# Two state decays ahead of the Silu in idle PSUM banks, with earlier x loads, earlier rows, the inverse deviation in PSUM and a hinted loop branch

## The chip, the cores and the metric

One NeuronCore of a Trainium2 chip runs the whole program, in fp32. The metric is the device time of one execution in microseconds (us). The kernel before takes 10367.23 us (median of 3 runs, 10365.2 to 10386.27).

## The reference

The input is 32 images of 256 x 256 positions with 4 features. What matters here is layer 0's mixer, a two-way Mamba. Behind it follow an expert layer, an attention and a routed MLP, which the second phase of the kernel computes.

```python
h = _L0_tok_ref(x, W, b)                      # tokens: 256 of width 256
h = concatenate([cls_tok, h], axis=1)         # 257 positions
h = h + _L0_attn_ref(_layernorm(h), ...)      # below

def _mamba_block(x, ...):                     # four of them, d=512, 16 states
    xn = _layer_norm(x, g, b)                 # 1 / sqrt(variance + eps)
    xs, z = split(xn @ in_w)
    xc = silu(conv(xs) + conv_b)              # 4 taps, depthwise
    delta = softplus(xc @ xd_w @ dtp_w + dtp_b)
    Bm, Cm = xc @ xB_w, xc @ xC_w
    dA = exp(delta[..., None] * A)            # the decays
    dBx = (delta * xc)[..., None] * Bm
    y = scan(h = dA * h + dBx; y = sum(h * C)) + D * xc
    return y * silu(z) @ out_w + x
fwd = blk(blk(x, 0), 1); bwd = blk(blk(x[:, ::-1], 2), 3)[:, ::-1]
concatenate([fwd, bwd]) @ merge_w
```

## The kernel before

Two phases run one after the other. `mamba_phase` computes tokens and the mixer, `tail_phase` the rest. The change lies in the first alone.

**Tiling.** The 32 images go in 16 groups of 2 (NB). A group needs four blocks, and each block of one group is a *job*: 64 jobs. The 512 channels are 4 chunks of 128 partitions (CI), so a job has 64 states (chunk c, state n; s = 16 c + n), each a tile of 128 x 512. A job is walked in 32 *units* u of two states (2u and 2u + 1). While a job's states are scanned, the engines also finish the job before (output projection) and prepare the next: normalisation, input projection, convolution, Silu, the projection xp, step sizes dt0 to dt3.

**Who does what.** ScalarE makes the decay of each state (`decays`, line 776) into one of two PSUM buffers (NDP = 2), so decay s waits for the scan of state s - 2. GpSimd multiplies B by u (`b_times_u`, lines 544 and 547) and for every fourth state C by h (line 556). VectorE scans (lines 978 and 982) and multiplies the other states by C (line 998), turns x - mean into the normalised value (`normalize`, line 944, which multiplies the tile cen by the tile rstd), and multiplies turned-back rows by the gate (`output`, line 1018). TensorE adds the states up in turned form (`add_state`, line 1233), turns a chunk's rows back (`channel_rows`, line 1245), and does all products (`product`, line 1117) and the tokens (`tokens`, line 1134). SyncE issues the DMAs.

**What sets the order.** Every engine has its own written order, `period(g, jj, first, last)`, with fixed units for each step (`gates_at`, `y_at`, `silu_at`, `norm_at`, CONV_AT = 15). The convolution's Silu (line 698, with a table load ahead and one behind, line 699) stands at u = 24 of ScalarE, after decay 51. The rows of chunks 0, 1 and 2 (y0, y1, y2) are turned back at u = 12 or 14, 18 and 25, at the head of the unit behind its two additions; VectorE takes them a unit later, between its scans. The products xp stand at u = 25 of TensorE, dt0 and dt1 at 26 and 27; ScalarE copies xp (line 707) at u = 26, starts softplus (lines 717 and 718) at 27 and takes logarithms (line 730) at 29 and 30; VectorE uses the first of these at u = 30 (line 953).

**Banks.** All products share three PSUM banks `w_ps` in turns. The turns are written in a list of keys (`preparation`, `one_job`, `later_keys`): turn i takes banks 0 and 1 when even, 2 and 1 when odd, y rows only one bank. A product waits until turn i - 2, for its second bank sometimes turn i - 1, is read (`bank_free`). `work_full` and `work_read`, one semaphore each for either parity, count the turns.

**The inverse deviation.** `inverse_deviation` (lines 656 and 659) takes a logarithm of the variance from PSUM into rstd in SBUF, tells that the turn "var" is read, and takes an exponential of half of it.

**Tokens.** In the job jj = 2 of a group (15 times) x of the next group is loaded (`load_x`, eight loads of 256 KB through two buffers, issued after the gates' products and the next weights) and turned into tokens at units 10 to 13 of TensorE: t0, then "var", y0, t1. ScalarE copies t1 (line 623) at u = 14, ahead of decay 32.

**The loop.** Job 0 stands ahead, then each engine has a loop of 15 passes over the four jobs jj = 1, 2, 3, 4; the last three jobs stand behind it (`run`).

Of the kernel before, what the change touches and what calls it, by code (L numbers as in the profile page):

```python
# [5 lines left out]
ALU = mybir.AluOpType  # L6
# [6 lines left out]
NB = 2  # L13
# [13 lines left out]
BLOCK_OF_JOB = (0, 2, 1, 3)  # L27
CONV_AT = 15
EPS = 1e-5
LOG_EXP = "natural_log_exp_and_others"  # L30
# [5 lines left out]
def mamba_phase(nc, a, h_mid, bc_dram, diag_dram, skip_dram):  # L36
# [13 lines left out]
    def preparation(jj, tokens):  # L50

        first = norm[:2] + ["t0"] + norm[2:] + ["t1"] if tokens else norm
        steps = first + conv + ["xp", "dt0", "dt1", "dt2", "dt3"]
        return [(name, 4 if name in ("t0", "t1") else jj) for name in steps]
# [98 lines left out]
    with ExitStack() as ctx:  # L153
# [94 lines left out]
        rstd_ready = sem("rstd_ready")  # L248
        xhat_ready = sem("xhat_ready")
        xn_ready = sem("xn_ready")  # L250
# [62 lines left out]
        def run(eng, lead_in, period, tail):  # L313

            lead_in()
            period(0, 0, True, False)
            with eng.Fori(0, GROUPS - 1) as g:
                for jj in (1, 2, 3, 4):
                    period(g, jj, False, False)
            for jj in (1, 2, 3):  # L320
                period(GROUPS - 1, jj, False, jj == 3)
            tail(GROUPS - 1)
# [4 lines left out]
        def _(sp):  # L327
# [63 lines left out]

            def load_x(g, jj):

                for n in range(8):
                    c, b, half = n // 4, n // 2 % 2, n % 2

                    if positive(g * 8 + 8 * (jj // 4) + n - 1):
                        sp.wait_ge(x_used, g * 8 + 8 * (jj // 4) + n - 1)
                    src = a["x"][bass.ds(g * NB + (jj // 4 * NB + b), 1), half * P:(half + 1) * P, c * P:(c + 1) * P, :]
                    sp.dma_start(x_in[:, n % 2, :, :], src.rearrange("o i j f -> (o i) j f")).then_inc(x_loaded[n % 2], 16)  # L400
# [33 lines left out]
            def period(g, jj, first, last):  # L434

                if not first:
                    sp.wait_ge(full_of("o1", g, jj - 1), nth("o1", g, jj - 1))
                load_out_w(jj)
                if jj == 4:

                    store_h(g)
                if not last:

                    sp.wait_ge(full_of("z3", g, jj), nth("z3", g, jj))
                    load_weights(jj + 1)
                    if jj == 2 and not is_final(g):
                        load_x(g, 4)
                    load_skip(g, jj + 1)
                    for c in range(CI):
                        load_diag(g, jj + 1, c)  # L450
                    bring_bc(g, jj + 1)
# [164 lines left out]
        def _(act):  # L616
# [34 lines left out]
            def inverse_deviation(kind, g, jj):  # L651

                name = "tvar" if kind == "tok" else "var"
                act.wait_ge(full_of(name, g, jj), nth(name, g, jj))
                w = banks(name, g, jj)
                func(rstd[:, :, :], w[:, :, 0:S], ACT.Ln, bias=eps_t[:, 0:1]).then_inc(read_of(name, g, jj), 1)

                act.wait_ge(read_of(name, g, jj), nth(name, g, jj))
                func(rstd[:, :, :], rstd[:, :, :], ACT.Exp, scale=-0.5).then_inc(rstd_ready, 1)

            def gain_and_bias(g, jj):
                k = BLOCK_OF_JOB[jj % 4]
                act.wait_ge(xhat_ready, job_count(g, jj, 1, 1))
                for c in range(CM):
                    last = func(xn[:, c, :, :], cen[:, c, :, :], ACT.Identity, scale=ln_g[:, k, c:c + 1],  # L665
                                bias=ln_b[:, k, c:c + 1])
                last.then_inc(xn_ready, 1)
# [95 lines left out]

            def decays(g, jj, s):

# [7 lines left out]

                if positive(job_count(g, jj, STATES, s + 1 - NDP)):
                    act.wait_ge(scan_done, job_count(g, jj, STATES, s + 1 - NDP))
                func(decay[:, s % NDP, :].rearrange("p (b t) -> p b t", b=NB), delta[:, c, :, 1:S], ACT.Exp,  # L776
# [37 lines left out]
            def prepare_back(g, jj):  # L814
                for c in (0, 2):
                    conv_input(g, jj, c)
                    conv_input(g, jj, c + 1)
                    conv_output(g, jj, c)
                    conv_output(g, jj, c + 1)
                conv_silu(g, jj)  # L820
                projections(g, jj)
# [81 lines left out]
            def lead(g, jj, s, last):  # L903

                if not (last and s >= STATES):
                    decays(g, jj, s)

            def period(g, jj, first, last):
                for u in range(UNITS):
# [3 lines left out]
                    after_even(g, jj, u, first, last)  # L913
                    lead(g, jj, NU * u + NDP + 1, last)
                    if u == silu_at(jj)[1]:
                        token_rows(g, jj, u // PAIRS - 1)
# [10 lines left out]
        def _(dve):  # L927
# [8 lines left out]
            def normalize(kind, g, jj):  # L936
                i = norms[kind, jj]
                dve.wait_ge(rstd_ready, g * 5 + i + 1)
                if kind == "tok" and jj:

                    dve.wait_ge(full_of("tvar", g, jj), nth("tvar", g, jj))
                dst = x_f if kind == "tok" else cen
                for c in range(CM):
                    last = dve.tensor_tensor(dst[:, c, :, :], cen[:, c, :, :], rstd[:, :, :], ALU.mult)
                last.then_inc(x0_ready if kind == "tok" else xhat_ready, 1)

# [16 lines left out]

            def scan(g, jj, s, b):
                inside = s not in POOL_C
# [10 lines left out]
                if s >= NST:  # L976

                    dve.tensor_tensor_scan(h, decay[:, s % NDP, :], bu[:, s % NBU, 0:NB * L], 0.0, ALU.mult, ALU.add  # L978
                                           ).then_inc(scan_done, 1)
# [66 lines left out]
            def period(g, jj, first, last):  # L1046
                for u in range(UNITS):
# [7 lines left out]
                    for b in range(NB if s < NST else 1):  # L1055
                        scan(g, jj, s, b)
                    if u - 1 in y_at(jj):
# [3 lines left out]
                    if size:  # L1061
                        step_size(*size, 0)
                    scan(g, jj, s + 1, 0)
                    if s + 1 in POOL_C and s < NST:
                        c_times_h(g, jj, s)
                        scan(g, jj, s + 1, 1)
                    else:
                        if s < NST:
                            scan(g, jj, s + 1, 1)
                        c_times_h(g, jj, s)  # L1070
                        if s + 1 not in POOL_C:
                            c_times_h(g, jj, s + 1)
                    if size:
                        step_size(*size, 1)
# [23 lines left out]
        def _(pe):  # L1098
# [176 lines left out]
            def period(g, jj, first, last):  # L1275
                for u in range(UNITS):
                    if u == 1 and not first:
                        channel_rows(g, jj - 1, 3)
                    if not (first and u == 0):
                        add_state(g, jj, NU * u - 2)  # L1280
                        add_state(g, jj, NU * u - 1)
                    if u in y_at(jj):
                        channel_rows(g, jj, y_at(jj).index(u))
                    if not first:
                        if u == 2:
# [31 lines left out]
                    elif step in (1, 2):  # L1317
                        conv(g, jj + 1, 0, part=[step - 1])
                    if step == 10:
                        projections(g, jj + 1)  # L1320
# [701 lines left out]
```

## Time and profile before

| | us |
|---|---|
| median of 3 runs | 10367.23 |
| the profiled execution | 10389.18 |
| its span, first to last instruction | 10387.4 |
| VectorE busy in the span | 8087.7 |
| TensorE busy | 8344.1 |
| GpSimd busy | 7059.5 |
| ScalarE busy | 5899.2 |

The profile is of one execution. Times in its timelines count from the first instruction. PE is TensorE's matmuls, PEld its weight loads, DVE VectorE, ACT ScalarE, POOL GpSimd, SP SyncE. "L998" is a line of the kernel, and `a<-b,c` says that tile a is written from tiles b and c. In brackets stands how long the engine was idle before the row, and who ended it; "issue" means that nothing in the profile explains the wait. A row with x2 merges two instructions. The state-space phase is some 8,600 us of the span.

### The profile page before, as it was taken

What the parts mean: (1) busy time and instruction counts of PE and PEld (TensorE: products, weight loads), DVE (VectorE), ACT (ScalarE), POOL (GpSimd) and SP (SyncE); (2) the same over time, 40 slices, a digit from 0 to 9 for tenths busy, and PEclk for the clock granted to TensorE, in tenths of its full rate; (3) what the DMA queues carried; (4) which work ended last, traced back from release to release, by engine and by line L of the source; (5) the groups of instructions that cost most, each with busy time, mean ns of one, the idle gap of its engine ahead of it and who ended that gap; (6) DMA issues with size and microseconds to landing.
All of it is one profiled execution on the core that took longest, in us unless ns stands there. A gap on an engine that the chain in (4) does not pass through costs nothing. (4 is left out here: it accounts for less than half of the span.)

```text
span 10387.4 us, 152898 instructions
## 1 busy us (share of the span) xinstructions
PE 8344.1 (80%) x42776; PEld 6881.5 (66%) x42776; DVE 8087.7 (78%) x10482; ACT 5899.2 (57%) x9202; POOL 7059.5 (68%) x7227
## 2 busy tenths in 40 slices
PE   5877777777878787878787877787877776999998
PEld 4666666666666666666666666676666664777776
DVE  4888889888988888888898888888888894333332
ACT  4565656565665666566566666665566662444443
POOL 4888888888888888888888888888888883000000
PEclk8888888888888888888888888888888887999998
DMA  2222222222222222222222222222222220000000
GB/s 93 94 89 99 92 98 91 99 92 93 92 94 93 90 98 93 90 79 90 89 98 93 98 91 97 93 98 92 90 93 96 92 90 25 11 10 10 12 9 9
DMA packets 414916, 819.68 MB, mean 79 GB/s; under 512 B 148919, under 2 KB 194139, under 8 KB 414043
## 3 DMA queue, kind: packets, MB, share of 16 engines
q1 hardware_dynamic: 410328, 806.69, 22.3%
q8 instruction: 359, 5.88, 0.2%
q14 instruction: 515, 4.21, 0.1%
q10 hardware_dynamic: 3714, 2.89, 0.1%
HBM read 783.16 MB, written 26.30 MB: 78 GB/s over the span
## 5 line engine op out<-in xcount | busy, mean ns | idle before, releaser
L776 ACT ACTIVATE decay<-delta,neg_a 128x512 f32<-128x512 f32 x4096 | 2793.0, 688 | 2484.5 <-DVE h_ps L978 1112.7
L544 POOL TENSOR_TENSOR bu<-b_all,u_buf 128x512 f32<-128x512 f32 x3072 | 3579.4, 1191 | 151.6 <-DVE h_ps L978 148.3
L978 DVE TENSOR_TENSOR_SCAN h_ps<-decay,bu 128x512 f32<-128x512 f32 x2304 | 2782.6, 1222 | 454.6 <-ACT decay L776 376.3
L1233 PE MATMUL y_ps<-ident,ch 128*128 128x128 f32 x16384 | 2579.9, 309 | 637.4 <-DVE ch L998 362.7
L1233 PEld LDWEIGHTS y_ps<-ident,ch 128*128 128x128 f32 x16384 | 2226.7, 161 | 1016.2 <-DVE ch L998 484.4
L556 POOL TENSOR_TENSOR ch<-ch,c_all 128x512 f32<-128x512 f32 x1024 | 1325.5, 1294 | 1112.1 <-DVE ch L978 910.0
L998 DVE TENSOR_TENSOR ch<-h_ps,c_all 128x512 f32<-128x512 f32 x3072 | 1977.2, 671 | 0.0
L547 POOL TENSOR_TENSOR bu<-b_all,u_buf 128x514 f32<-128x514 f32 x1024 | 1245.6, 1237 | 66.8 <-issue 56.3
L1117 PE MATMUL w_ps<-xn,in_w 128*128 128x257 f32 x4096 | 1074.8, 408 | 170.5 <-ACT xn L665 83.6
L982 DVE TENSOR_TENSOR_SCAN h_ps<-decay,bu 128x256 f32<-128x256 f32 x1536 | 1046.7, 737 | 125.3 <-POOL bu L547 98.2
L1117 PEld LDWEIGHTS w_ps<-xn,in_w 128*128 128x128 f32 x4096 | 799.9, 206 | 320.2 <-issue 81.1
L1576 POOL TENSOR_TENSOR rstd_F<-h_F 128x514 f32<-128x514 f32 x16 | 17.5, 1095 | 1429.1 <-DMA h_F<-h_mid 1429.1
L978 DVE TENSOR_TENSOR_SCAN ch<-decay,bu 128x512 f32<-128x512 f32 x768 | 926.2, 1206 | 55.4 <-ACT decay L776 54.0
L1117 PE MATMUL w_ps<-xs_pad,diag_store 128*128 128x257 f32 x4096 | 950.9, 380 | 0.0
L1117 PEld LDWEIGHTS w_ps<-xs_pad,diag_store 128*128 128x128 f32 x4096 | 746.5, 190 | 91.3
L1117 PE MATMUL w_ps<-dtbc,dt_w 32*128 32x257 f32 x1024 | 443.4, 551 | 247.9 <-ACT dtbc L707 127.6
L1117 PE MATMUL w_ps<-sz,out_w 128*128 128x257 f32 x2048 | 507.4, 391 | 119.1 <-ACT x_b L762 59.1
L1117 PEld LDWEIGHTS w_ps<-sz,out_w 128*128 128x128 f32 x2048 | 379.6, 193 | 182.8 <-ACT x_b L762 66.5
L1226 PE MATMUL y_ps<-skip_diag,xc 128*128 128x128 f32 x2048 | 347.4, 324 | 172.6 <-ACT y_t L751 172.5
L1117 PEld LDWEIGHTS w_ps<-dtbc,dt_w 32*128 32x128 f32 x1024 | 216.2, 246 | 391.6 <-ACT rstd L718 184.7
L1226 PEld LDWEIGHTS y_ps<-skip_diag,xc 128*128 128x128 f32 x2048 | 317.1, 232 | 215.8 <-ACT y_t L751 211.0
L1245 PE MATMUL w_ps<-ident,y_t 128*128 128x128 f32 x1024 | 187.5, 314 | 259.1 <-ACT y_t L751 259.1
(258 smaller groups left out, 11583.9 us busy)
## 6 DMA issues: line engine op xcount, KB each, us to landing
b_all<-bc_dram SPq DMA_DIRECT2D x512, 514.0 KB, 8.6
c_all<-bc_dram SPq DMA_DIRECT2D x512, 514.0 KB, 10.0
in_w<-in_L_attn_in_w SPq DMA_DIRECT2D x64, 1024.0 KB, 5.0
diag_store<-diag_dram SPq DMA_DIRECT2D x256, 256.0 KB, 2.9
x_in<-in_x SPq DMA_DIRECT2D x128, 256.0 KB, 2.6
out_w<-in_L_attn_out_w SPq DMA_DIRECT2D x64, 512.0 KB, 3.9
skip_diag<-skip_dram SPq DMA_DIRECT2D x64, 256.0 KB, 4.1
h_mid<-h_cur SPq DMA_DIRECT2D x32, 257.0 KB, 2.2
```

Of the source, the lines that this page charges most:

```text
L544: pool.tensor_tensor(bu[:, s % NBU, 0:NB * L].rearrange("p (b t) -> p b t", b=NB), b_all[:, n // NU, n % NU, :, 1:], u_buf[:, c % 2, :, 1: ...
L547: pool.tensor_tensor(bu[:, s % NBU, :], b_all[:, n // NU, n % NU, :, :].rearrange("p b s -> p (b s)"), u_buf[:, c % 2, :, :].rearrange("p ...
L556: pool.tensor_tensor(h, h, c_all[:, n // NU, n % NU, :, 1:], ALU.mult).then_inc(pool_c_done, 1)
L776: func(decay[:, s % NDP, :].rearrange("p (b t) -> p b t", b=NB), delta[:, c, :, 1:S], ACT.Exp, scale=neg_a[:, k, c, n:n + 1]).then_inc(dec ...
L978: dve.tensor_tensor_scan(h, decay[:, s % NDP, :], bu[:, s % NBU, 0:NB * L], 0.0, ALU.mult, ALU.add).then_inc(scan_done, 1)
L982: last = dve.tensor_tensor_scan(h[:, cols], decay[:, s % NDP, cols], bu[:, s % NBU, b * S + 1:(b + 1) * S], bu[:, s % NBU, b * S:b * S + 1 ...
L998: dve.tensor_tensor(ch[:, s % NPR, :].rearrange("p (b t) -> p b t", b=NB), h_ps[:, h_slot(s), :].rearrange("p (b t) -> p b t", b=NB), c_al ...
L1117: last = pe.matmul(w[0:rows, b, 0:S], lhs, rhs, start=(i == 0), stop=(i == len(terms(b)) - 1))
L1226: pe.matmul(y_ps[:, k, :], xc[:, jj % 2, c, b, 1 + half * P:1 + (half + 1) * P], skip_diag[:, jj % 2, c, :], start=(k == 0), stop=False, s ...
L1233: last = pe.matmul(y_ps[:, k, :], ch[:, s % NPR, k * P:(k + 1) * P], ident[:, :], is_transpose=True, start=False, stop=(n == NST - 1 and k ...
L1245: last = pe.matmul(w[:, k * P:(k + 1) * P], y_t[:, k, :], ident[:, :], is_transpose=True, start=True, stop=True, skip_group_check=True)
L1576: pool.tensor_tensor(rstd[s][:, :, :], h[s][:, 0, :, :], h[s][:, 1, :, :], ALU.add).then_inc(h_summed[s], 1)
```

## The change

- **Early decays.** A key "early" joins the list of turns between cv3 and xp. ScalarE writes the decays of states 52 and 53 into its two banks at u = 24, ahead of the copy of y and the Silu. VectorE scans these two states from there, and after the scan of state 53 says that the turn is read. Decays 54 and 55 go to the usual buffers and wait for the scans of 50 and 51. In the lead-in, and in the last job, nothing is early.
- **x loads.** The first two of the eight loads are issued at the head of SyncE's job, the six others where all were.
- **y1.** The rows of chunk 1 are turned back at the end of TensorE's unit 17, not in unit 18 behind the additions of states 34 and 35.
- **Inverse deviation.** For the blocks (not for the tokens) logarithm and exponential are written into the banks of "var" themselves, VectorE multiplies from there, and says only then that the turn is read.
- **Branch hint.** The loops are made with `hint_back_edge=True`.

```diff
@@ -26,6 +26,7 @@
 CONV_AT = 15
+EARLY = 2 * (CONV_AT + 9) + 4, 2 * (CONV_AT + 9) + 5
 EPS = 1e-5
@@ -50,7 +51,7 @@
         first = norm[:2] + ["t0"] + norm[2:] + ["t1"] if tokens else norm
-        steps = first + conv + ["xp", "dt0", "dt1", "dt2", "dt3"]
+        steps = first + conv + ["early", "xp", "dt0", "dt1", "dt2", "dt3"]
         return [(name, 4 if name in ("t0", "t1") else jj) for name in steps]
@@ -246,7 +247,7 @@
         rstd_ready = sem("rstd_ready")
-        xhat_ready = sem("xhat_ready")
+        rstd_logs = sem("rstd_logs")
         xn_ready = sem("xn_ready")
@@ -314,7 +315,7 @@
             period(0, 0, True, False)
-            with eng.Fori(0, GROUPS - 1) as g:
+            with nc.Fori(0, GROUPS - 1, engines=[eng.engine], hint_back_edge=True) as g:
                 for jj in (1, 2, 3, 4):
@@ -389,9 +390,9 @@
-            def load_x(g, jj):
-                for n in range(8):
+            def load_x(g, jj, part=range(8)):
+                for n in part:
                     c, b, half = n // 4, n // 2 % 2, n % 2
@@ -433,6 +434,8 @@
+                if jj == 2 and not is_final(g):
+                    load_x(g, 4, range(2))
                 if not first:
@@ -444,7 +447,7 @@
                     if jj == 2 and not is_final(g):
-                        load_x(g, 4)
+                        load_x(g, 4, range(2, 8))
                     load_skip(g, jj + 1)
@@ -653,6 +656,12 @@
                 w = banks(name, g, jj)
+                if kind == "job":
+                    func(w[:, :, 0:S], w[:, :, 0:S], ACT.Ln, bias=eps_t[:, 0:1]).then_inc(rstd_logs, 1)
+                    act.wait_ge(rstd_logs, job_count(g, jj, 1, 1))
+                    func(w[:, :, 0:S], w[:, :, 0:S], ACT.Exp, scale=-0.5).then_inc(rstd_ready, 1)
+                    return
                 func(rstd[:, :, :], w[:, :, 0:S], ACT.Ln, bias=eps_t[:, 0:1]).then_inc(read_of(name, g, jj), 1)
@@ -660,7 +669,7 @@
                 k = BLOCK_OF_JOB[jj % 4]
-                act.wait_ge(xhat_ready, job_count(g, jj, 1, 1))
+                act.wait_ge(read_of("var", g, jj), nth("var", g, jj))
                 for c in range(CM):
@@ -761,7 +770,19 @@
-            def decays(g, jj, s):
+            def early_decays(g, jj):
+                k = BLOCK_OF_JOB[jj % 4]
+                w = banks("early", g, jj + 1)
+                for c in (2, 3):
+                    act.wait_ge(read_of(f"cv{c}", g, jj + 1), nth(f"cv{c}", g, jj + 1))
+                for i, s in enumerate(EARLY):
+                    c, n = s // NST, s % NST
+                    func(w[:, i, :].rearrange("p (b t) -> p b t", b=NB), delta[:, c, :, 1:S], ACT.Exp,
+                         scale=neg_a[:, k, c, n:n + 1]).then_inc(decays_ready, 1)
+                act.sem_inc(full_of("early", g, jj + 1), 1)
+            def decays(g, jj, s, behind=0):
@@ -771,8 +792,8 @@
-                if positive(job_count(g, jj, STATES, s + 1 - NDP)):
-                    act.wait_ge(scan_done, job_count(g, jj, STATES, s + 1 - NDP))
+                if positive(job_count(g, jj, STATES, s + 1 - NDP - behind)):
+                    act.wait_ge(scan_done, job_count(g, jj, STATES, s + 1 - NDP - behind))
                 func(decay[:, s % NDP, :].rearrange("p (b t) -> p b t", b=NB), delta[:, c, :, 1:S], ACT.Exp,
@@ -817,6 +838,9 @@
                     conv_output(g, jj, c + 1)
+                act.wait_ge(read_of("cv3", g, jj), nth("cv3", g, jj))
+                act.sem_inc(full_of("early", g, jj), 1)
+                act.sem_inc(read_of("early", g, jj), 1)
                 conv_silu(g, jj)
@@ -902,8 +926,11 @@
+                if not last and s in EARLY:
+                    return
                 if not (last and s >= STATES):
-                    decays(g, jj, s)
+                    decays(g, jj, s, behind=NDP if not last and s - NDP in EARLY else 0)
@@ -912,6 +939,8 @@
                     lead(g, jj, NU * u + NDP + 1, last)
+                    if NU * u + 2 * NDP in EARLY and not last:
+                        early_decays(g, jj)
                     if u == silu_at(jj)[1]:
@@ -940,9 +969,10 @@
                 dst = x_f if kind == "tok" else cen
+                inverse = rstd[:, :, :] if kind == "tok" else banks("var", g, jj)[:, :, 0:S]
                 for c in range(CM):
-                    last = dve.tensor_tensor(dst[:, c, :, :], cen[:, c, :, :], rstd[:, :, :], ALU.mult)
-                last.then_inc(x0_ready if kind == "tok" else xhat_ready, 1)
+                    last = dve.tensor_tensor(dst[:, c, :, :], cen[:, c, :, :], inverse, ALU.mult)
+                last.then_inc(x0_ready if kind == "tok" else read_of("var", g, jj), 1)
@@ -961,7 +991,18 @@
-            def scan(g, jj, s, b):
+            def decay_of(g, jj, s, last):
+                if s in EARLY and not last:
+                    return banks("early", g, jj + 1)[:, EARLY.index(s), :]
+                return decay[:, s % NDP, :]
+            def early_read(g, jj):
+                dve.wait_ge(scan_done, job_count(g, jj, STATES, EARLY[-1] + 1))
+                dve.sem_inc(read_of("early", g, jj + 1), 1)
+            def scan(g, jj, s, b, last):
                 inside = s not in POOL_C
@@ -975,7 +1016,7 @@
-                    dve.tensor_tensor_scan(h, decay[:, s % NDP, :], bu[:, s % NBU, 0:NB * L], 0.0, ALU.mult, ALU.add
+                    dve.tensor_tensor_scan(h, decay_of(g, jj, s, last), bu[:, s % NBU, 0:NB * L], 0.0, ALU.mult, ALU.add
                                            ).then_inc(scan_done, 1)
@@ -1053,23 +1094,25 @@
                     for b in range(NB if s < NST else 1):
-                        scan(g, jj, s, b)
+                        scan(g, jj, s, b, last)
                     if u - 1 in y_at(jj):
                         step_size(*size, 0)
-                    scan(g, jj, s + 1, 0)
+                    scan(g, jj, s + 1, 0, last)
                     if s + 1 in POOL_C and s < NST:
                         c_times_h(g, jj, s)
-                        scan(g, jj, s + 1, 1)
+                        scan(g, jj, s + 1, 1, last)
                     else:
                         if s < NST:
-                            scan(g, jj, s + 1, 1)
+                            scan(g, jj, s + 1, 1, last)
                         c_times_h(g, jj, s)
                             c_times_h(g, jj, s + 1)
+                    if s in EARLY and not last:
+                        early_read(g, jj)
                     if size:
@@ -1279,8 +1322,10 @@
                         add_state(g, jj, NU * u - 1)
-                    if u in y_at(jj):
+                    if u in y_at(jj)[::2]:
                         channel_rows(g, jj, y_at(jj).index(u))
+                    if u == y_at(jj)[1] and last:
+                        channel_rows(g, jj, 1)
                     if not first:
@@ -1316,6 +1361,8 @@
                         conv(g, jj + 1, 0, part=[step - 1])
+                    if u == y_at(jj)[1] - 1:
+                        channel_rows(g, jj, 1)
                     if step == 10:
```

## Rows read from the trace of the kernel before

**Rows 1.** The page, part 1: busy us (share of the span) and instructions of each engine.

```profile
PE 8344.1 (80%) x42776; PEld 6881.5 (66%) x42776; DVE 8087.7 (78%) x10482; ACT 5899.2 (57%) x9202; POOL 7059.5 (68%) x7227
```

**Rows 2.** A window of the state-space phase: length; PE, PEld, DVE, ACT, POOL busy; clock; DMA.

```profile
3000.00:5000.00 2000.00, 1582.91 (x8346) 1325.22 (x8344) 1772.60 (x2183) 1204.27 (x1871) 1642.90 (x1679) 0.86 0.26 93
```

**Rows 3.** VectorE's waits: waited for whom, us in total, times, longest us.

```profile
DVE h_ps L978 <- ACT decay L776: 376.3, 251, 3.4
DVE sz L1018 <- PE w_ps L1245: 240.9, 162, 7.8
```

**Rows 4.** Timeline of VectorE around the Silu: start, us, what, [idle before, releaser].

```profile
3185.25 1.23 DVE L978 TENSOR_TENSOR_SCAN h_ps<-decay,bu 128x512 f32<-128x512 f32 x1 [3.35 <-ACT decay L776]
3186.39 0.67 DVE L1018 TENSOR_TENSOR sz<-w_ps,sz 128x512 f32<-128x512 f32 x1
3187.39 1.22 DVE L978 TENSOR_TENSOR_SCAN ch<-decay,bu 128x512 f32<-128x512 f32 x1 [0.33 <-ACT decay L776]
...
3189.11 2.34 DVE L978 TENSOR_TENSOR_SCAN h_ps<-decay,bu 128x512 f32<-128x512 f32 x2
...
3200.62 0.72 DVE L953 SCALAR_TENSOR_TENSOR diag_store<-diag_store 128x514 f32<-128x514 f32 x1 [0.58 <-ACT sp_l L730]
```

**Rows 5.** Timeline of ScalarE, the same stretch.

```profile
3179.29 0.59 ACT L751 ACTIVATE y_t<-y_ps 128x512 f32<-128x512 f32 x1
...
3184.43 1.30 ACT L776 ACTIVATE decay<-delta,neg_a 128x512 f32<-128x512 f32 x2
...
3189.28 0.58 ACT L707 ACTIVATE dtbc<-w_ps 64x514 f32<-64x514 f32 x1
...
3192.11 0.67 ACT L717 ACTIVATE diag_store<-w_ps,dtp_b 128x514 f32<-128x514 f32 x1
...
3193.80 0.69 ACT L776 ACTIVATE decay<-delta,neg_a 128x512 f32<-128x512 f32 x1 [0.43 <-DVE h_ps L978]
```

**Rows 6.** Timeline of TensorE, the same stretch.

```profile
3181.80 0.60 PE L1245 MATMUL w_ps<-ident,y_t 128*128 128x128 f32 x4
3183.18 3.68 PE L1117 MATMUL w_ps<-xc,xp_w 128*64 128x257 f32 x16 [0.77 <-ACT xc L698]
3186.79 1.09 PE L1233 MATMUL y_ps<-ident,ch 128*128 128x128 f32 x8
3189.90 1.13 PE L1117 MATMUL w_ps<-dtbc,dt_w 32*128 32x257 f32 x4 [2.02 <-ACT dtbc L707]
```

**Rows 7.** GpSimd's waits, then VectorE's timeline at a turn and before the last jobs.

```profile
POOL bu L547 <- issue: 56.3, 14, 4.2
...
2945.07 1.40 DVE L982 TENSOR_TENSOR_SCAN h_ps<-decay,bu 128x256 f32<-128x256 f32 x2 [5.03 <-POOL bu L547]
...
8293.46 1.39 DVE L982 TENSOR_TENSOR_SCAN h_ps<-decay,bu 128x256 f32<-128x256 f32 x2
```

**Rows 8.** VectorE's groups (busy, mean ns, idle), then min/median/max of line 944.

```profile
L944 DVE TENSOR_TENSOR cen<-cen,rstd 128x514 f32<-128x514 f32 x128 | 119.9, 975 | 36.4 <-ACT rstd L659 36.4
...
L1029 DVE TENSOR_TENSOR h_cur<-h_cur,w_ps 128x514 f32<-128x514 f32 x32 | 21.9, 684 | 38.2 <-PE w_ps L1117 38.2
...
L944 DVE TENSOR_TENSOR cen<-cen,rstd x128: 680/802/1751, 95.6 to 8478.2; 128x514 f32<-128x514 f32 x128
```

**Rows 9.** Timelines of TensorE and VectorE in a job that makes tokens.

```profile
3121.64 3.80 PE L1134 MATMUL w_ps<-tok_ident,x_in 128*128 128x128 f32 x16
...
3133.88 3.90 PE L1134 MATMUL w_ps<-tok_ident,x_in 128*128 128x128 f32 x16
...
3143.54 3.60 PE L1233 MATMUL y_ps<-ident,ch 128*128 128x128 f32 x16 [0.28 <-PE w_ps L1134]
...
3137.57 1.48 DVE L944 TENSOR_TENSOR cen<-cen,rstd 128x514 f32<-128x514 f32 x2
```

**Rows 10.** Timelines of ScalarE and VectorE behind the second convolution chunk.

```profile
3161.63 0.69 ACT L692 ACTIVATE xc<-w_ps,conv_b 128x514 f32<-128x514 f32 x1 [2.90 <-PE w_ps L1117]
...
3162.93 1.22 DVE L978 TENSOR_TENSOR_SCAN ch<-decay,bu 128x512 f32<-128x512 f32 x1 [0.15 <-ACT decay L776]
```


## The prediction

> **What bounds the kernel now.** I read the page first: VectorE is busy 78% of the span, TensorE 80% [rows 1], but TensorE's share is an average of two phases. A window inside the state-space (Mamba) phase shows VectorE at 1772.6 of 2000 us, TensorE at 1582.9, GpSimd at 1642.9 [rows 2]. So in this phase VectorE, which runs the scans, is the nearest to a bound, and what can be won there is its 11% of idle time. The list of VectorE's waits then says who ends that idle time: ScalarE's decays for 376.3 us, TensorE's turned-back rows (y) for 240.9 us [rows 3]. The timeline says where, and it repeats nearly alike in all 64 jobs: a gap of 3.35 us before state 52 (the decays stand behind the convolution's Silu), smaller ones before the y rows, and 5.0 us at each turn of the loop.
>
> **Early decays, with their bank turn.** There are 63 jobs that prepare a next one. Now: VectorE is done with state 51 at 3181.90 (3.35 us of idle time before 3185.25), scans state 52 at 3185.25, takes y2 at 3186.39, scans state 53 at 3187.39 and state 54 at 3189.11 [rows 4]. The engine that makes it wait is ScalarE: from its copy of y at 3179.29 to the next decay at 3184.43 it takes 5.14 us for the copy, two table loads and the Silu [rows 5].
>
> After the change, decays 52 and 53 (1.30 us for two, rows 5) stand before that copy. State 52 can be scanned at 3181.85, 3.4 us earlier. But three things move back:
> - The copy of y starts at 3180.6, so y2, whose four transposes ended at 3182.40 [rows 6], ends at 3183.7. VectorE wants it at 3183.0 and waits 0.7. State 53 follows 1.0 later (as 3186.39 to 3187.39 in rows 4), at 3184.75, and ends at 3186.0. State 54 is scanned at about 3186.5, still 2.6 us ahead of before; its decay comes at 3184.43 + 1.30 = 3185.73 and does not hold it.
> - The new turn "early" takes a pair of banks, and the projection xp has the next turn of the same parity. TensorE's first xp product now waits for VectorE's scan of state 53: 3186.0, not 3183.18 [rows 6]. Queued behind it on TensorE are the additions of states 50 and 51 and dt0. xp with the additions took from 3183.18 to 3186.79 and another 1.09 [rows 6]; so ScalarE gets xp at about 3189.7 (before: copied at 3189.28, rows 5), TensorE is free at 3190.7 and dt0 (1.13, rows 6) ends at 3191.8.
> - ScalarE, in order, holds decay 56 behind the copy of xp, and decay 58 behind the softplus of dt0. That softplus starts at 3191.8 instead of 3192.11; decay 58 follows without the 0.43 us of idle time that it has now: 0.7 us ahead of 3193.80 [rows 5].
>
> From there ScalarE works without a pause until the logarithm for which VectorE waits at 3200.62 [rows 4]. So of 3.4 us only **0.7 us a job** comes through: 63 x 0.7 = 44 us. What is late next is the chain Silu, xp, dt0, softplus; I expect the stall to reappear at states 56 to 60. Bounds: nothing or a loss of 1.3 us if the chain had no slack, 3.68 us (3.35 + 0.33, rows 4) if it had enough.
>
> **Back-edge hint.** Entering the body again costs VectorE 5.03 us of idle time before its first scan; the same place ahead of the last three jobs, which are not in the loop, has none [rows 7]. GpSimd shows it as 56.3 us of "issue" in 14 pieces [rows 7], so there are 14 such turns (15 passes). If the hint does what its name says, the gap goes: 14 x 5.0 = **70 us**. Bounds: nothing, and 70. I take all of it, because the place without a branch goes on with no gap at all. What the hint itself costs no row shows; I take nothing and keep the range for it.
>
> **Inverse deviation in PSUM.** Two effects.
> - The normalisation reads cen and the deviation. From SBUF both, one takes 975 ns on average over 128; the same kind of instruction with one operand in PSUM takes 684 [rows 8]. 128 x 0.29 = 37 us. In most jobs VectorE leads there, in some TensorE's queue is what counts; I take three quarters, **27 us**. Bounds: 0 and 37. The two ScalarE instructions keep their number and their size; I cost them at nothing.
> - The pair of banks of "var" is now free only after VectorE's normalisation, not after ScalarE's logarithm. In the job that also turns x into tokens (15 of them) the second token product t1 has the next turn of that parity. Now it starts at 3133.88; the normalisation ends at 3139.05 [rows 9]. TensorE stands for 5.1 us, with the additions of states 24 to 29 and t1's second half queued behind. What it has in hand: the 16 transposes at 3143.54 took 3.60 us where a group of 8 takes 1.09 [rows 6, 9], so 1.4 us of waiting, and 0.3 us of idle time before them. That leaves 3.4 us: ScalarE waits longer for t1 with decays 32 and 33 behind, VectorE stalls at state 32. 15 x 3.4 = **51 us lost**. Bounds: 0 and 5.1 x 15 = 77.
>
> The Trainium skill has a rule that speaks against this part: by VectorE: DVE Perf Modes, section on the trn2 errata, a source in PSUM costs VectorE 120 cycles of fixed time against 58 from SBUF, at 0.96 GHz some 65 ns more an instruction. By it the 128 instructions would be an estimated 8 us slower, not 27 faster. The trace doesn't agree as far as it goes: the fastest normalisation from SBUF and the instructions that read PSUM lie within 4 ns (680 and 684, rows 8), and the dear ones are dear only from SBUF.
>
> **Rows of chunk 1 sooner.** The transposes (y1) go ahead of the additions of states 34 and 35: one group of 8, some 0.9 us sooner (such a group takes 1.09 with its tail, rows 6). VectorE's wait there shrinks. But two states on, it stands anyway: ScalarE gets conv 1 from TensorE at 3161.63, after 2.90 us of waiting, and the decay behind it reaches VectorE's scan only at 3162.93 [rows 10]. TensorE's order up to the end of conv 1 has the same work in it. I cost it at **nothing** (bounds 0 and 0.9 x 63 = 57 us won).
>
> **First two loads of x sooner.** They take two issues on SyncE's queue ahead of out_w, which is needed two units later. TensorE starts the tokens at 3121.64 with no idle time before it [rows 9]: x was there. Load 2 still waits for the first tile to be used. **Nothing.**
>
> **Sum.** -70 - 44 - 27 + 51 = -90 us. The profiled execution took 10389.2 us (span 10387.4), so 10299; the median of the runs shown is 22 us lower, so **10277 us**.
>
> **Rivals.**
> - *The Silu's stall goes in full* (xp is not held as I think, or softplus has more slack): 63 x (3.68 - 0.7) = 188 us more, 10089; half of it, 10183. For it: VectorE's wait is 3.35 us in every job. Against: the turn in the same pair of banks. Chance 0.14.
> - *The hint does nothing*: the gap of 5.0 us stays, 10347. For it: no row shows a hint at work. Against: GpSimd and VectorE both show the gap at the turn and at no other place, and the turn is what the hint names. Chance 0.12.
> - *PSUM is no cheaper to read*, the dear normalisations have another cause: 27 us are not won, 10304. The page named above is the rule for this. Chance 0.08.
> - *y1 does come through*: 10277 - 57 = 10220. Chance 0.08.
> - *Slower*: ScalarE's chain from the Silu on is what sets the job, and the two decays ahead of it cost their 1.30 us whole. 63 x (1.3 + 0.7) = 126 us over the forecast, 10403. It decides from 1.8 us a job over the forecast on, that is, once decay 58 starts later than 3194.9 in the rows' terms. For it: ScalarE has no idle time between decay 58 and the logarithm. Chance 0.08.
> - The forecast: 0.50.
>
> **Range.** From half of the Silu's stall to the hint doing nothing: 10183 to 10347. A measurement of this kernel can tell about 0.2% (21 us) from no change, so faster means below 10346. Faster takes the forecast and the three rivals that end below it or a little above: 0.80; within 0.2%, which the hint's rival gives: 0.12; slower: 0.08.
>
> **What would show it.** Right: no idle time of VectorE at the loop's turn and no "issue" before GpSimd's bu; state 52 scanned with no wait, and waits at y2 and at states 56 to 60 in its place; the first xp product released by VectorE; normalisations at 0.69 us; in the token job TensorE idle before t1 until the normalisation, ScalarE's wait for t1 4 us longer; y1's wait gone and a wait of about 1 us at state 41. Wrong: a job that is over 1.5 us shorter from the Silu alone, "issue" still there at the turn, or no new wait before t1.

## The result, and the profile after

| | us |
|---|---|
| before, median of 4 runs | 10366.22 |
| after, median of 4 runs | 10441.2 (10435.98 to 10454.33) |
| ratio | 1.0071, 95% interval [1.0054, 1.0089] |
| forecast | 10277, range 10183 to 10347 |

The changed kernel is 0.7% slower. The forecast was 164 us off and on the wrong side.

The profiled execution of the changed kernel has a span of 10452.5 us. Line numbers moved: 978 is now 1019, 998 is 1039, 776 is 797, 1018 is 1059, 1117 is 1160. The state-space phase looks much as it did [rows 2], with VectorE a little less busy. First its window, then VectorE's waits [rows 3]:

```profile
3000.00:5000.00 2000.00, 1560.81 (x8230) 1297.23 (x8228) 1746.85 (x2153) 1195.75 (x1864) 1620.09 (x1666) 0.86 0.26 92
```

```profile
DVE h_ps L1019 <- ACT decay L797: 482.6, 369, 5.2
...
DVE sz L1059 <- PE w_ps L1288: 277.2, 189, 7.8
...
DVE ch L1019 <- ACT decay L797: 87.6, 107, 1.2
```

The decays keep VectorE waiting 106 us longer than before, and the turned-back rows 36 us longer. The forecast had both a little shorter. Where the wait is now shows in the timeline of VectorE around the Silu [rows 4], in a job of the same place in its group:

```profile
3211.35 1.22 DVE L1019 TENSOR_TENSOR_SCAN h_ps<-w_ps,bu 128x512 f32<-128x512 f32 x1
3214.04 0.69 DVE L1059 TENSOR_TENSOR sz<-w_ps,sz 128x512 f32<-128x512 f32 x1 [1.46 <-PE w_ps L1288]
3215.06 1.22 DVE L1019 TENSOR_TENSOR_SCAN ch<-w_ps,bu 128x512 f32<-128x512 f32 x1 [0.33 <-POOL bu L547]
3216.20 0.67 DVE L1039 TENSOR_TENSOR ch<-h_ps,c_all 128x512 f32<-128x512 f32 x1
3216.79 2.34 DVE L1019 TENSOR_TENSOR_SCAN h_ps<-decay,bu 128x512 f32<-128x512 f32 x2
3219.03 1.27 DVE L1039 TENSOR_TENSOR ch<-h_ps,c_all 128x512 f32<-128x512 f32 x2
3224.46 1.23 DVE L1019 TENSOR_TENSOR_SCAN h_ps<-decay,bu 128x512 f32<-128x512 f32 x1 [4.16 <-ACT decay L797]
```

States 52 and 53 are scanned from w_ps, and 52 with no wait: the 3.35 us gap is gone. VectorE waits 1.46 us for y2, and 4.16 us at state 56; over all 63 jobs the wait for y2 is 1.65 us on average. TensorE in the same stretch [rows 6], and windows of it (length; PE, PEld, DVE, ACT, POOL busy; the granted clock behind them):

```profile
3210.69 1.16 PE L1269 MATMUL y_ps<-skip_diag,xc 128*128 128x128 f32 x8 [2.22 <-ACT y_t L760]
3211.69 1.46 PE L1276 MATMUL y_ps<-ident,ch 128*128 128x128 f32 x8
3212.94 1.06 PE L1288 MATMUL w_ps<-ident,y_t 128*128 128x128 f32 x4
3216.49 6.56 PE L1160 MATMUL w_ps<-xc,xp_w 128*64 128x257 f32 x16 [2.49 <-DVEq L1003]
3222.98 1.09 PE L1276 MATMUL y_ps<-ident,ch 128*128 128x128 f32 x8
3224.01 1.13 PE L1160 MATMUL w_ps<-dtbc,dt_w 32*128 32x257 f32 x4
```

```profile
3207.60:3210.70 3.10, 0.88 (x9) 0.64 (x7) 2.80 (x3) 3.04 (x6) 3.10 (x4) 1.00 0.00 0
3210.70:3214.00 3.30, 3.30 (x20) 2.90 (x20) 1.88 (x3) 3.27 (x3) 3.00 (x8) 0.72 0.00 0
3214.00:3216.50 2.50, 0.01 (x2) 0.04 (x1) 2.13 (x3) 2.47 (x3) 1.15 (x2) 0.50 0.01 3
3216.50:3223.00 6.50, 6.50 (x17) 3.38 (x17) 3.80 (x5) 0.00 (x0) 5.70 (x5) 0.55 0.01 3
3223.00:3227.00 4.00, 4.00 (x25) 2.98 (x24) 2.54 (x3) 3.60 (x7) 0.13 (x1) 1.00 0.14 46
```

xp is released by line 1003, VectorE's word that state 53 is scanned, as forecast. But its 8 products, which the profile shows as 16 instructions, take 6.56 us where they took 3.68 [rows 6]. In 45 of the 64 jobs they take 5.3 us, in 18 from 6.0 to 6.6, in one 3.65. Between two idle stretches, 2.22 and 2.49 us, the granted clock falls from 1.00 (2.4 GHz) to 0.50 (1.2 GHz), and xp runs at 0.55. In the kernel before, TensorE was idle for 1.00 and 0.77 us in the same places, and the clock behind them stayed at 1.00:

```profile
3179.93 1.16 PE L1226 MATMUL y_ps<-skip_diag,xc 128*128 128x128 f32 x8 [1.00 <-ACT y_t L751]
```

```profile
3183.20:3186.90 3.70, 3.70 (x17) 2.18 (x18) 1.65 (x2) 2.91 (x4) 1.98 (x5) 1.00 0.00 0
```

After the change ScalarE stands behind xp for 6.68 us [rows 5]:

```profile
3215.18 1.30 ACT L797 ACTIVATE decay<-delta,neg_a 128x512 f32<-128x512 f32 x2
3223.17 0.59 ACT L716 ACTIVATE dtbc<-w_ps 64x514 f32<-64x514 f32 x1 [6.68 <-PE w_ps L1160]
3223.66 1.28 ACT L797 ACTIVATE decay<-delta,neg_a 128x512 f32<-128x512 f32 x2
```

The other parts did what was forecast. At the loop's turn VectorE goes on without a gap [rows 7], the normalisations take 683 ns [rows 8], and in the token job TensorE waits for them ahead of t1 [rows 9]. VectorE's timeline at a turn, its group of line 974, TensorE's wait in total:

```profile
2972.32 1.39 DVE L1023 TENSOR_TENSOR_SCAN h_ps<-decay,bu 128x256 f32<-128x256 f32 x2
```

```profile
L974 DVE TENSOR_TENSOR cen<-cen,w_ps 128x514 f32<-128x514 f32 x128 | 82.1, 683 | 38.0 <-ACT w_ps L663 38.0
```

```profile
PE w_ps L1177 <- DVE cen L974: 74.3, 15, 5.0
```

### The profile page after: what moved, and what is told of

Read it like the earlier page. It is cut to its first block and busy times, and to the rows that moved or that the text cites. A ratio compares the mean times of both kernels' runs of the same rounds, so it can differ in the third digit from the quotient of the medians.

```text
span 10452.5 us, 152924 instructions
## 1 busy us (share of the span) xinstructions
PE 8324.6 (80%) x42776; PEld 6829.8 (65%) x42776; DVE 8058.8 (77%) x10482; ACT 5877.4 (56%) x9202; POOL 7028.1 (67%) x7227
## 5 line engine op out<-in xcount | busy, mean ns | idle before, releaser
L797 ACT ACTIVATE decay<-delta,neg_a 128x512 f32<-128x512 f32 x3970 | 2702.1, 687 | 2159.1 <-DVE h_ps L1019 940.3
L1019 DVE TENSOR_TENSOR_SCAN h_ps<-decay,bu 128x512 f32<-128x512 f32 x2241 | 2711.2, 1223 | 545.2 <-ACT decay L797 482.6
L1276 PE MATMUL y_ps<-ident,ch 128*128 128x128 f32 x16384 | 2481.7, 301 | 573.0 <-DVE ch L1039 423.6
L1276 PEld LDWEIGHTS y_ps<-ident,ch 128*128 128x128 f32 x16384 | 2125.8, 156 | 930.2 <-DVE ch L1039 564.2
L1019 DVE TENSOR_TENSOR_SCAN ch<-decay,bu 128x512 f32<-128x512 f32 x705 | 849.6, 1205 | 82.2 <-ACT decay L797 81.9
L1160 PE MATMUL w_ps<-dtbc,dt_w 32*128 32x257 f32 x1024 | 420.0, 531 | 100.9 <-ACT rstd L727 98.4
L1160 PE MATMUL w_ps<-xc,xp_w 128*64 128x257 f32 x1024 | 359.6, 528 | 158.0 <-DVEq L1003 153.8
```

The lines of the kernel that those rows point to most:

```text
L1019: dve.tensor_tensor_scan(h, decay_of(g, jj, s, last), bu[:, s % NBU, 0:NB * L], 0.0, ALU.mult, ALU.add).then_inc(scan_done, 1)
L1160: last = pe.matmul(w[0:rows, b, 0:S], lhs, rhs, start=(i == 0), stop=(i == len(terms(b)) - 1))
L1276: last = pe.matmul(y_ps[:, k, :], ch[:, s % NPR, k * P:(k + 1) * P], ident[:, :], is_transpose=True, start=False, stop=(n == NST - 1 and k ...
```

## The experiments

**Theory A**: the early decays made the kernel slower, through xp: released late by the held banks, then run at the low clock. **Rival B**: they are near even, and the loss is in the banks that the deviation holds. **Rival C**: the late release counts, the clock is a bystander. Each time below is a median, and each ratio is to the kernel before as measured beside that experiment; its medians there were 10371.66, 10374.93 and 10376.17 us.

### The change without its early decays

The diff above without every line that names "early", EARLY, `early_decays`, `early_read`, `decay_of` or `behind`.

> The change without its early decays (hint, x loads, y1, deviation in PSUM stay). Theory A, the chain behind the Silu: the early decays are what made the kernel slower, about 2.2 us in each of 63 jobs, since xp waits for the scan of state 53 and TensorE, idle before it, works at 1.2 GHz; without them 10441 - 138 = about 10303 us, 0.6% below the kernel before. Rival B, the loss comes from the banks of the deviation held longer and the early decays are near even: about 10440.

Measured 10329.41 us, ratio 0.9962 [0.995, 0.9975]. The other parts together gain 42 us, the early decays then lose 112. B falls. The gain is 26 us short of the expectation. VectorE's waits in this run are:

```profile
DVE h_ps L987 <- ACT decay L784: 465.4, 336, 5.1
DVE sz L1027 <- PE w_ps L1254: 169.9, 115, 7.9
```

With the early decays (the changed kernel) the first is 482.6 us and the second 277.2. So the stall at state 52, 3.35 us a job, came back almost whole at state 56, some 3.1 us on average, and the longer wait for turned-back rows, y2 above all, came on top: 107 us.

### The branch hint alone

```diff
-            with eng.Fori(0, GROUPS - 1) as g:
+            with nc.Fori(0, GROUPS - 1, engines=[eng.engine], hint_back_edge=True) as g:
```

> The kernel before with the branch hint alone. Both theories: the gap of 5.0 us of VectorE at 14 turns goes, 10366 - 70 = about 10296 us. If the other parts of the change are what took that gap away, 10366.

Measured 10290.91 us, ratio 0.9922 [0.9906, 0.9939]: 81 us less, 5.8 a turn. "issue" is gone from GpSimd's waits [rows 7]. The forecast looked at VectorE and GpSimd alone; at each of the 14 turns TensorE stood too, for nothing that the profile shows. At the turn of rows 7:

```profile
2945.03 0.47 PE L1233 MATMUL y_ps<-ident,ch 128*128 128x128 f32 x1 [5.19 <-issue]
2949.47 1.65 PE L1233 MATMUL y_ps<-ident,ch 128*128 128x128 f32 x7 [3.97 <-issue]
```

### The early decays alone

The kernel before with the lines that the first experiment left out.

> The kernel before with the early decays alone. Theory A: xp released by VectorE after state 53, at a granted clock of 0.5 to 0.7 and 5.4 to 6.4 us long in place of 3.68; VectorE's stall of 3 to 4 us now at state 56; 10366 + 140 = about 10505 us. Rival B: xp at 3.7 us, no stall over 1.5 us behind the Silu, about 10320 us.

Measured 10446.57 us, ratio 1.0075 [1.0058, 1.0092]: 75 us more, half of what was expected. The sign and the place are A's, the size is not. TensorE's group of xp tells why (busy, mean ns, idle before), for the kernel before, this one, and the whole change:

```profile
L1117 PE MATMUL w_ps<-xc,xp_w 128*64 128x257 f32 x1024 | 237.4, 384 | 52.5 <-ACT xc L698 52.5
```

```profile
L1151 PE MATMUL w_ps<-xc,xp_w 128*64 128x257 f32 x1024 | 323.1, 486 | 158.0 <-DVEq L994 153.8 <-ACT xc L699 4.2
```

```profile
L1160 PE MATMUL w_ps<-xc,xp_w 128*64 128x257 f32 x1024 | 359.6, 528 | 158.0 <-DVEq L1003 153.8 <-ACT xc L707 4.2
```

Over 64 jobs xp took 3.7, 5.0 and 5.6 us. The idle time before it is the same 153.8 us in the last two, yet xp took 36.5 us more in the whole change. With the early decays alone it took 3.7 us in 13 jobs, 5.3 in 49 and 6.6 in 2; in the whole change 3.7 in 1, 5.3 in 45 and 6.0 to 6.6 in 18. The 36.5 us are about the size of the difference between 75 us alone and 112 on top of the rest (37). That they are its cause, and which of the other parts lowers the clock further, was not tried.

### The inverse deviation in PSUM alone

The lines of the diff in `inverse_deviation`, `gain_and_bias` and `normalize`.

> The kernel before with the inverse deviation in PSUM alone. Theory A: normalisations at 0.69 us, 37 us less of which some 27 come through, and t1 released later in the 15 jobs with tokens, 4.5 us each, 68 us; together about +40, 10407 us. Rival B: the held banks cost over 100 us, 10470 or more.

Measured 10403.19 us, ratio 1.0032 [1.002, 1.0043]: 31 us more. As A had it, and no more.

### Unused products in TensorE's two waits

```diff
+                    if u == y_at(jj)[2] and not last:
+                        bank_free("y2", g, jj, 0)
+                        for n in range(8):
+                            pe.matmul(banks("y2", g, jj)[:, 0:P], ident[:, :], ident[:, :], start=True, stop=True,
+                                      skip_group_check=True)
...
                     if step == 10:
+                        for n in range(9):
+                            pe.matmul(y_ps[:, 0, :], zeros[:, :], ident[:, :], start=False, stop=False,
+                                      skip_group_check=True)
                         projections(g, jj + 1)
```

The first eight write into y2's own bank ahead of y2. The nine others add zeros to y.

> The whole change, with 8 unused products put into TensorE's wait for the copy of y and 9 products of zeros into its wait before xp; no other order is touched. Theory A with the clock in it: xp starts where it did but runs at a granted clock near 1 and takes 3.7 us in place of 5.4 to 6.4, and VectorE's stall at state 56 falls by 1.7 to 2.7 us: 10441 - 63 x 2.0 = about 10315 us. Rival C, the clock is a bystander and only the release after state 53 counts: 10441 or more.

Measured 10268.36 us, ratio to the kernel before 0.9904 [0.9883, 0.9924]: 173 us less than the whole change, for 17 products a job that compute nothing, and 47 us more than was expected. C falls. TensorE, then VectorE:

```profile
3140.50 0.60 PE L1290 MATMUL w_ps<-ident,y_t 128*128 128x128 f32 x4
3140.93 2.17 PE L1375 MATMUL y_ps<-ident,zeros 128*128 128x128 f32 x18
3143.59 3.65 PE L1162 MATMUL w_ps<-xc,xp_w 128*64 128x257 f32 x16 [0.48 <-DVEq L1005]
```

```profile
3141.14 0.69 DVE L1061 TENSOR_TENSOR sz<-w_ps,sz 128x512 f32<-128x512 f32 x1 [0.62 <-PE w_ps L1290]
...
3148.65 1.23 DVE L1021 TENSOR_TENSOR_SCAN h_ps<-decay,bu 128x512 f32<-128x512 f32 x1 [1.19 <-ACT decay L799]
```

xp waits for VectorE as before, but takes 3.65 us. The wait for y2 is 0.62 us and the stall at state 56 is 1.19: the forecast's own timetable (0.7 us, and a stall from state 56 on) holds once the clock does. The nine products show as x18, since such a product in fp32 is two instructions. Over the whole run xp took 236.2 us, 123 less than in the changed kernel. Against the change without its early decays this run is 61 us faster (10329 to 10268): with the clock kept up the early decays gain about what the forecast gave them, 44 us. That the added products helped nowhere else was not tried.

### The halves of xp released one by one

```diff
             def bank_free(name, g, jj, b):
+                if name == "xp" and b == 0 and not (isinstance(g, int) and jj == 0):
+                    pe.wait_ge(scan_done, job_count(g, jj - 1, STATES, EARLY[0] + 1))
+                    return
```

> The whole change, but the first half of xp (its first bank) waits for the scan of state 52 only, the second half for that of 53 as before. If the held banks are what makes xp late, xp starts at the end of the Silu, 2.5 us sooner, and its stall goes with it: 63 x 2.5 = 160 us less, about 10280; with the clock kept up on top, 10180. If the chain is late for another reason (the Silu 1.3 us later), no more than 40 us less.

Measured 10207.81 us, ratio 0.984 [0.9821, 0.9859]: 233 us less than the whole change, between the two expectations and nearer to the one with the clock kept up. In the job shown TensorE has one long idle stretch left, 2.22 us:

```profile
3125.56 1.16 PE L1272 MATMUL y_ps<-skip_diag,xc 128*128 128x128 f32 x8 [2.22 <-ACT y_t L760]
3126.55 1.04 PE L1279 MATMUL y_ps<-ident,ch 128*128 128x128 f32 x8
3127.43 0.60 PE L1291 MATMUL w_ps<-ident,y_t 128*128 128x128 f32 x4
3128.87 3.68 PE L1163 MATMUL w_ps<-xc,xp_w 128*64 128x257 f32 x16 [0.84 <-ACT xc L707]
```

xp now follows the Silu by itself, here and in 31 of the 64 jobs, and takes 3.68 us there. In the 32 others it starts straight behind y2, and takes 4.3 to 4.5 us, with up to 0.52 us of waiting between its halves. Over all jobs xp took 249.8 us, against 359.6 with the whole change. So the one wait of one bank on the wrong state cost the late release and most of xp's clock with it. The transposes of y2 are still slow in some jobs: VectorE's wait for y2 is 1.34 us on average, not 0.62. Against the change without its early decays (10329) this is 122 us less, more than the forecast gave them.

### The copy of y ahead of the early decays

```diff
+                    if u == silu_at(jj)[1]:
+                        token_rows(g, jj, u // PAIRS - 1)
                     if NU * u + 2 * NDP in EARLY and not last:
                         early_decays(g, jj)
-                    if u == silu_at(jj)[1]:
-                        token_rows(g, jj, u // PAIRS - 1)
```

> The whole change, with ScalarE's copy of y ahead of the two early decays. VectorE's wait for y2 (1.2 to 2.6 us) goes, the scan of state 53 and so xp come 1.7 us sooner: 63 x 1.7 = 107 us less, 10334 us, if the clock stays as low as it is. If only the wait for y2 goes and xp is bound by something else, the stall at 56 grows by as much and the time stays 10441.

Measured 10326.83 us, ratio 0.995 [0.9933, 0.9966]: 114 us less than the whole change. The number is the one expected, but its condition did not hold: the clock did not stay as low as it was. xp took 314.6 us over all jobs instead of 359.6, so up to 45 of the 114 us are the clock's, and the agreement is in part luck.

### Both edits together

> The two edits together: y copied ahead of the early decays, and the halves of xp released one by one. Theory A: one idle stretch of about 2 us on TensorE is left, xp starts at the Silu's end; the chain is then 1.3 us later than without early decays while VectorE has up to 3.4 us less to wait. About 2.5 us a job better than the change without early decays (10329): 10175 us. If the Silu's chain keeps all, 10329 + 63 x 1.3 = 10410.

Measured 10216.5 us, ratio 0.985 [0.9831, 0.9868]: no better than the halves alone, and 41 us short of the expectation. With y copied first the idle time of TensorE lies in one piece before xp, and xp is slow again in part: 5.3 us in 29 of the 63 jobs behind the first, after an idle stretch of 2.0 us. An instruction takes 441 ns on average, against 393 with the halves alone:

```profile
L1163 PE MATMUL w_ps<-xc,xp_w 128*64 128x257 f32 x1024 | 285.9, 441 | 132.3 <-ACT xc L707 132.3
```

### The deviation in PSUM, but not in the job that makes tokens

```diff
-                if kind == "job":
+                if kind == "job" and jj % 4 != 3:
```

(and `gain_and_bias` and `normalize` by the same condition, with rstd and a semaphore of their own).

> The kernel before with the inverse deviation in PSUM, but from SBUF as before in the one job of four that also makes tokens. If the held banks ahead of t1 are what made the deviation in PSUM slower (+31 us), VectorE's 5.0 us stall at state 32 goes and the gain of the other three jobs stays: 3.0 us a group in the trace, 15 groups, 45 us below the kernel before, 10326 us. If the dearer normalisation in SBUF was never worth anything, 10372.

Measured 10348.0 us, ratio 0.9975 [0.9964, 0.9985]: 28 us less than the kernel before, where the deviation in PSUM in all jobs was 31 us more. So the banks held ahead of t1 cost 60 us, 4.0 us in each of the 15 jobs, less whatever the cheaper normalisations gain there; the gain of the other three jobs is smaller than expected.

### The x loads and the rows of chunk 1 alone

The hunks of `load_x`, and of `channel_rows` in TensorE's period.

> The kernel before with the two x loads first and the rows of chunk 1 sooner, nothing else. The prediction cost both at nothing: VectorE's wait for y1 falls by 0.85 us and comes back at state 41 behind the second convolution chunk; tokens start when they did: 10372 within 15 us. If y1 comes through, 10372 - 55.

Measured 10378.38 us, ratio 1.0004 [0.9995, 1.0012]: nothing. VectorE's waits show the swap against 240.9 us for y [rows 3]:

```profile
DVE sz L1020 <- PE w_ps L1247: 180.0, 122, 7.9
DVE ch L980 <- ACT decay L778: 109.7, 168, 1.2
```

The kernel before has 54.0 us in the second of these rows: 61 us less for y, 56 more for decays.

```profile
DVE ch L978 <- ACT decay L776: 54.0, 161, 0.7
```

### The whole change with both mends, and with eight unused products

The halves of xp released one by one, the token job's deviation in SBUF; then the first eight unused products on top.

> The whole change with xp's halves released one by one and with the token job's deviation in SBUF: 10208 less what the token job lost, 15 x 4.5 = 68 us: about 10140 us. If the two interact (the token job's stall moves to the Silu), 10208.

Measured 10141.66 us, ratio 0.9777 [0.9764, 0.9789]: 1.7 us from the expectation.

> The same with 8 unused products in TensorE's wait for the copy of y. If the wait for y2 (1.25 to 1.44 us in split, 0.63 in warm) is the clock's doing, it falls to 0.63 us and up to 63 x 0.7 = 44 us go with it: 10096 us; if what follows is bound by ScalarE anyway, 10140.

Measured 10101.93 us, ratio 0.974 [0.9728, 0.9753]. 40 us less, where up to 44 were expected. It beats the kernel before by 2.6% and the changed one by 3.2%. In the window from 3000 to 5000 us VectorE is busy 91%, and the clock is 0.89:

```profile
3000.00:5000.00 2000.00, 1618.84 (x8884) 1364.73 (x8883) 1824.67 (x2252) 1245.72 (x1942) 1693.73 (x1738) 0.89 0.27 94
```

## Why the prediction was wrong

The step that failed is the second point of the early decays: "xp with the additions took from 3183.18 to 3186.79 and another 1.09". The sum moved xp's start 2.8 us back and kept its duration, 3.6 us, from a row where TensorE had been idle for 1.00 and 0.77 us and the clock was 1.00. In the changed kernel TensorE is idle for 2.22 and 2.49 us just before, the clock falls to 0.50, and xp takes 5.6 us on average. The same sum with the duration that the changed trace shows would have given a loss of some 1.2 us a job (5.6 - 3.7 - 0.7). The first point had the same fault in small: it took y2's transposes, too, at their old speed. The wait for y2 was priced at 0.7 us and measured 1.65 on average (0.6 to 0.7 in 16 of the 63 jobs, 1.5 to 2.3 in the others). With these 0.95 us the sum comes to a loss of some 2.2 us a job; measured were 1.8 (112 / 63).

| term | forecast | measured |
|---|---|---|
| early decays | -44 | +75 alone, +112 on the rest |
| hint | -70 | -81 |
| deviation in PSUM, gain | -27 | -28 (three jobs of four) |
| deviation in PSUM, t1 | +51 | +60 |
| y1 and x loads | 0 | +2, within the noise |

Point by point: VectorE's scan of 52 without a wait, y2's wait, the release of xp by state 53, and the stall from state 56 on came as written. y2's wait was 1.46 us instead of 0.7 in the job shown, since the transposes too ran at the lower clock (1.06 us for four, 0.60 before). The slower rival had the right sign and the wrong mechanism: it put the loss on the Silu's 1.3 us. With xp's halves released one by one the Silu is as late and the kernel is faster, so those 1.3 us are not it. The hint gave more than VectorE's gap of 5.0 us showed. TensorE stood there for itself, 5.19 and 3.97 us, and no longer does; whether that is the rest of the 81 us was not tried. The parts measured one by one do not add up to the whole: -81 + 75 + 31 + 2 is +27, and the whole change is +75. The early decays cost 37 us more beside the other parts.

VectorE: DVE Perf Modes of the Trainium skill, trn2 errata, made a PSUM source dearer. The trace does not bear that out here: all 128 lie between 679 and 694 ns with PSUM, and between 680 and 1751 from SBUF. The 32 normalisations of the tokens, which still read both tiles from SBUF, keep a median of 1414 ns. The Trainium skill's SBUF — State Buffer, section "Who interferes with whom", has the reason that fits: a VectorE instruction with two SBUF inputs contends with a GpSimd instruction that reads SBUF. That GpSimd is the cause was not tried here.

The Trainium skill, TensorE: Matmul & The Clock Gate, section on HAM oscillation, describes this: a TensorE that waits before every group of products is throttled, and starts the next group slow. The trace agrees: the granted clock goes from 1.00 to 0.50, and an instruction of xp takes 528 ns on average against 384 before. The waits here, 2.2 and 2.5 us, are shorter than those of the page's case. It should have been one of the rivals.

## What to carry to other kernels

When a change makes TensorE wait, price the products behind the wait at both clock levels; the wait may cost more after it than in it. Filling spare PSUM banks with other engines' data is only as cheap as the next turn of these banks: ask who wants them next, and release each bank by itself. A change of several parts that looks bad may be mostly good: here two edits to what waits for what turned a loss of 0.7% into a gain of 2.2%.

## What was not expected of the hardware

- Products that compute nothing, put into 2.2 and 2.5 us of idle time, made the kernel 173 us faster (10441 to 10268).
- After the same idle time of 2.4 to 2.5 us xp is not always slow: it kept its 3.7 us in 13 of 64 jobs with the early decays alone, and in one with the whole change. Behind stretches of 1.00 and 2.03 us, in the run with both edits, it was slow in 29 of the 63 jobs after the first; behind 1.00 and 0.77 us, in the kernel before, in none of them. What decides in a single job was not settled.
- A branch back over a long body stopped VectorE for 5.03 us and TensorE for 5.19 and 3.97, and the hint took VectorE's gap away whole: no idle time is left before its first scan.
